# The first layer's neighbour sums of a graph kernel: from gathered rows to an edge-count matrix times a table in SBUF

## The chip, the cores and the metric

The kernel runs on one core of one Trainium2 chip, in one launch. The metric is the time of that launch on the device in microseconds (us), the median of three runs. Engines are named as in the profile: PE (TensorE matmuls), PEld (its weight loads), DVE (VectorE), ACT (ScalarE), POOL (GpSimd) and SP (SyncE, which here only issues DMAs; its rows are marked SPq).

## The reference, cut to what matters

The input is a graph with 6250 nodes, a feature row `x` of 256 floats for each node, and 206250 directed edges sorted by their destination `dst`. Two graph layers follow each other, and each has a small feed-forward part behind it. The change touches the first graph layer alone:

```python
# layer 0; feat = layernorm(x)
t1    = feat @ W1
msg   = t1[src] + feat[src] * feat[dst] @ W2
msg   = msg / (sqrt(out_deg[src]) * sqrt(out_deg[dst]))[:, None]
agg   = segment_sum(msg, dst)
embed = where(in_cnt > 0, t1 + agg, 0) + b        # leaky relu, divided by its norm
x     = x + embed
x     = x + (layernorm(x) @ Wf.T + bf)            # layer 0's feed-forward part
# layer 1: m = clifford(h[src] * r[edge_type]) * gate * norm, summed by dst, and so on
```

Every term of `agg` is linear in the source's row, and `feat[dst]` is the same for all edges of a destination. So the kernel needs for each destination only the sum, over its edges, of one table row of the source, `feat[src] / sqrt(out_deg[src])`, and a count. All multiplications with W1 and W2 come behind that sum. Layer 1 can't do this: there each edge has its own factor, the relation row `r[edge_type]`.

## The kernel before, in words

The 6250 nodes lie in 49 blocks of 128 (`NB`), node 128b + p on partition p. Each block of destinations has a window of `C` = 35 slots of 128 edges, found at run time, so there are 49 x 35 = 1715 slots a layer (`SLOTS`). A group is seven slots (`SG`); a block has five groups (`SPB`).

**Start.** DVE finds where the blocks' windows begin (L1260 to L1281), and builds one-hots for a histogram of the sources, which PE adds up (L1293 and L693); that gives the out-degrees. SP loads the edge windows (L502). Then DVE and ACT write the table (L1329, L1081), and SP stores it to HBM as `t1_d` (L510).

**First pass** (`first_pass` on PE, ACT and DVE). For each slot POOL gathers 128 table rows by an indirect DMA (`gathers`, L630) into one of 18 buffers, and after each six gathers it clears a scratch tile (L627). DVE makes a 128 x 128 f32 one-hot of the destinations (`pick_edges`, L1366), and PE multiplies the two in f32 into the block's sum in PSUM (`aggregate`, L736). Beside it the edges are put in order of their relation for layer 1: DVE ranks them (`marks`, `places`), makes one-hots of the target slot and lane (`sends`, L1449 and L1453), ACT scales the small ones by three payloads (L1109), PE moves the edges with them (`move`, L760), and `in_place` writes the result. Some groups after a block's sum is complete, its node work follows in small steps: `features`, `turn_features`, `messages`, `embeddings`, `embed_norm`, `residual`, `ffn_input`, `turn_ffn`, `feed_forward`, `fed` and `table_row`, which writes the rows of layer 1's table. X, all of x, stays in SBUF throughout.

**Second pass.** Layer 1 again gathers (POOL), multiplies each row with a relation row that PE looks up (L717, L1383), adds up by destination, and so on; behind it a top-k search and the last sum.

Each engine runs a list written out by hand: the calls in the loop over n in its `first_pass` are its order, and semaphores named `s_...` tie the lists together. A call that waits holds back all that stands behind it on its engine.

## Time and profile before

| | us |
|---|---|
| median of 3 runs | 5443.28 (5443.25 to 5448.71) |
| span of the profiled execution | 5537.5 |
| PE busy | 3805.9 (69% of the span) |
| DVE busy | 3132.6 (57%) |
| ACT busy | 1618.8 (29%) |
| POOL busy | 3849.2 (70%) |

The profiled execution is another one than the three timed runs. The page gives no time for it beside its span, which is 94.2 us above the median. Sums below are made in the time of the span, and only a difference is carried over to the median.

The first gather of layer 0 begins at 245.37 us of the span, and the last row of layer 1's table is written at 2830.9 us: the first pass takes 2586 us, the second with its end the remaining 2706 us.

### The profile page before, as it was taken

The numbers are of one execution on the slowest core, as the hardware profiler recorded it, in microseconds if no ns is written. First come the engines' busy times: TensorE is split into PE (matmuls) and PEld (weight loads), VectorE is DVE, ScalarE is ACT, GpSimd is POOL, SyncE is SP. The second block draws the span as 40 slices with busy tenths as digits, with TensorE's granted clock in tenths as the row PEclk, the third lists the DMA queues.
The fourth block names the chain that finished last, engine by engine and source line by source line (L and its number), as shares of the span: only waits on it lengthen the run. The fifth ranks groups of instructions, "written<-read, shape, count | busy, mean of one in ns | idle before, by whom it ended". The sixth has DMA issues, their size and how long they took to land.

```text
span 5537.5 us, 68744 instructions
## 1 busy us (share of the span) xinstructions
PE 3805.9 (69%) x19471; PEld 2905.8 (52%) x19471; DVE 3132.6 (57%) x12068; ACT 1618.8 (29%) x6417; POOL 3849.2 (70%) x4302
## 2 busy tenths in 40 slices
PE   6555555555556555555557887888788888888886
PEld 6444444444444444444445665656566666665654
DVE  8756565665655656555555555555455555555545
ACT  3144444544444444444420111111111111111111
POOL 0177776777777777776757777777777777777772
PEclk9577777777777777777779989999999998999988
DMA  4333333333333333333334444444444444444443
GB/s 97 117 94 97 93 99 92 99 94 98 98 97 96 96 98 93 96 95 94 95 104 116 113 111 111 113 115 112 110 115 110 115 114 110 111 110 114 112 108 76
DMA packets 278430, 572.85 MB, mean 103 GB/s; under 512 B 88622, under 2 KB 167790, under 8 KB 278056
## 3 DMA queue, kind: packets, MB, share of 16 engines
q0 software_dynamic: 164640, 456.82, 31.9%
q1 hardware_dynamic: 101576, 103.13, 6.9%
q10 hardware_dynamic: 11840, 8.50, 0.5%
q8 instruction: 164, 2.69, 0.2%
q14 instruction: 210, 1.72, 0.1%
HBM read 541.27 MB, written 26.92 MB: 103 GB/s over the span
## 4 chain that ended last, share of the span: by engine, by line
PE 42%; DVE 31%; another core or an unknown queue 16%; issue 9%; DMA 1%; ACT 0%; SPq 0%; DVEq 0%; PEldq 0%; ACTq 0%
PE psE L736 18%; DVE both L1366 8%; PE psY L717 6%; PE psT L717 6%; DVE work L1453 5%; DVE work L1449 4%; PE psE L936 3%; PE psE L917 3%; DVE work L1293 2%; PE psY L693 1%; DVE work L1383 1%; DMA acc_d<-work 1%; DVE work L1374 1%; PE psE L872 1%
## 5 line engine op out<-in xcount | busy, mean ns | idle before, releaser
L630 POOL DMA_INDIRECT work<-t_d,srci x3430 | 3271.3, 954 | 1587.8 <-issue 1155.8
L736 PE MATMUL psE<-work,both 128*128 128x257 f32 x6860 | 2219.4, 448 | 875.8 <-issue 373.7
L736 PEld LDWEIGHTS psE<-work,both 128*128 128x128 f32 x6860 | 1388.0, 225 | 1242.5 <-issue 469.2
L1109 ACT ACTIVATE work<-work 128x35 f16<-128x35 bf16 x5145 | 1133.5, 311 | 692.0 <-DVE work L1449 440.9
L1366 DVE TENSOR_SCALAR both<-iof,dstf 128x128 f32<-128x128 f32 x3430 | 813.7, 345 | 47.8 <-issue 25.7
L1449 DVE TENSOR_SCALAR work<-iob,work 128x35 bf16<-128x35 bf16 x1715 | 273.3, 269 | 806.4 <-remote 668.9
L1383 DVE TENSOR_TENSOR work<-work,psY 128x257 f32<-128x257 f32 x857 | 347.5, 420 | 631.1 <-PE psY L717 206.5
L1383 DVE TENSOR_TENSOR work<-work,psT 128x257 f32<-128x257 f32 x858 | 348.0, 420 | 601.1 <-PE psT L717 214.6
L717 PE MATMUL psT<-relb,work 126*128 126x257 bf16 x2574 | 452.1, 286 | 21.2 <-DVE work L1374 19.1
L717 PE MATMUL psY<-relb,work 126*128 126x257 bf16 x2577 | 459.8, 290 | 0.5 <-issue 0.5
L627 POOL MEMSET work<- 128x640 bf16 x571 | 380.2, 666 | 0.2
L1453 DVE TENSOR_SCALAR work<-iob,work 128x128 f16<-128x128 bf16 x1715 | 346.9, 321 | 21.0 <-issue 20.7
L717 PEld LDWEIGHTS psT<-relb,work 126*128 126x128 bf16 x2574 | 261.5, 102 | 183.8 <-issue 26.3
L717 PEld LDWEIGHTS psY<-relb,work 126*128 126x128 bf16 x2577 | 265.8, 103 | 166.3 <-issue 27.6
L917 PE MATMUL psE<-accf,work 128*128 128x256 f32 (+1 forms) x800 | 188.2, 383 | 8.3 <-DVE rstd L1517 4.3
L627 POOL MEMSET accf<- 128x640 bf16 x285 | 193.2, 678 | 0.1
L1200 ACT ACTIVATE accf<-psE,score 128x256 f32<-128x256 f32 x49 | 23.2, 473 | 568.0 <-PE psE L936 239.1
L1374 DVE TENSOR_SCALAR work<-work,tid 126x640 bf16<-126x640 f16 (+3 forms) x493 | 169.2, 388 | 13.7 <-DMA work<-types_d 13.6
L760 PE MATMUL psY<-work 128*128 128x105 f16 x1715 | 137.6, 217 | 55.5 <-issue 45.6
L693 PE MATMUL psY<-work 125*128 125x49 bf16 x1650 | 158.7, 269 | 18.1 <-DVE work L1293 17.2
L917 PEld LDWEIGHTS psE<-accf,work 128*128 128x128 f32 x800 | 149.4, 196 | 30.7 <-DVE rstd L1517 6.1
L760 PEld LDWEIGHTS psY<-work 128*128 128x128 f16 x1715 | 115.2, 102 | 95.9 <-issue 64.6
(262 smaller groups left out, 3291.1 us busy)
## 6 DMA issues: line engine op xcount, KB each, us to landing
work<-t_d,srci POOLq DMA_INDIRECT x3430
work<-types_d SPq DMA_DIRECT2D x245, 220.5 KB
both<-acc_d SPq DMA_DIRECT2D x98, 130.0 KB
t_d<-accf SPq DMA_DIRECT2D x7, 910.0 KB, 9.3
acc_d<-work ACTq DMA_DIRECT2D x1, 6370.0 KB
t_d<-accf SPq DMA_DIRECT2D x49, 130.0 KB
X<-in_x SPq DMA_DIRECT2D x1, 6144.0 KB
out<-X SPq DMA_DIRECT2D x6, 896.0 KB
```

The lines of the kernel that those rows point to most:

```text
L627: pool.memset(idle[layer], 0.0).then_inc(s_pause, 1)
L630: pool.indirect_dma_start(gath[:, n % RG, :], None, table, bass.IndirectOffsetOnAxis(ap=srci[:, n:n + 1], axis=0)).then_inc(s_g[n % RG], 16)
L717: ins = nc.tensor.matmul(psR[n % BANKS][:, 0:DW], oht[0:PT, g % 2, at, :], relb[0:PT, part, c, 0:DW], start=((c, part) == (mine[0][0], 0)) ...
L736: ins = nc.tensor.matmul(psE[:, b % 2, 0:DW], sel[:, third, k % SG, :], gath[:, n % RG, 0:DW], start=False, stop=(k == C - 1))
L760: ins = nc.tensor.matmul(psY[:, b % 2, 0:3 * C], to_q[:, n % 2, k % SG, :], to_s3[:, n % 2, k % SG, :, :].rearrange("p j s -> p (j s)"), s ...
L917: ins = nc.tensor.matmul(bank[:, i * D:i * D + many * P].rearrange("p (q n) -> p q n", n=P), f1[:, t, ht * P:ht * P + P], rows[:, t, :, :] ...
L1109: ins = nc.scalar.activation(to_s3[:, n % 2, i, j, :], to_s[:, n % 2, i, :], ACT.Copy, scale=load3[:, b // RB % 2, j, w:w + 1])
L1366: ins = v.tensor_scalar(sel[:, n % 3, i, :], iof[:, :], dstf[:, k + i:k + i + 1], None, ALU.is_equal)
L1374: ins = v.tensor_scalar(oht[0:PT, n % 2, at:at + many, :], types[0:PT, n % 2, first:first + many, :], tid[0:PT, c:c + 1], None, ALU.is_equal)
L1383: v.tensor_tensor(rows, rows, psR[n % BANKS][:, 0:DW], ALU.mult).then_inc(s_po, 1)
L1449: ins = v.tensor_scalar(to_s[:, n % 2, i, :], iob[:, 0:C], spot_s[:, b // RB % 2, w + i:w + i + 1], None, ALU.is_equal)
L1453: ins = v.tensor_scalar(to_q[:, n % 2, i, :], iob[:, :], spot_q[:, b // RB % 2, w + i:w + i + 1], None, ALU.is_equal)
```

## The change

Layer 0's gathers, the one-hots `pick_edges(0, ...)` and the f32 matmuls with them are gone. In their place:

- **A count matrix.** A block of 128 destinations is cut into 16 windows of 8 nodes (`WINS`, `NODES`). SP loads for each window up to 384 edges as three runs of 128, destinations and sources apart, from copies of both lists padded at the end (`windows`: 32 small DMAs a block). After a turn by PE (`turn_window`), DVE makes one-hots for four windows at once (`edge_hots`): of the source's low seven bits, 128 wide, and of (destination, source's block), 8 x 49 = 392 wide. PE multiplies the two (`histogram`, three matmuls a window), which gives for 8 destinations and 6272 sources how many edges join them. ACT copies the counts as bf16 into the matrix `adj` (`counts_out`).
- **The table in SBUF.** The table is no longer read from HBM. While it is made, each row is split into three bf16 parts whose sum is the f32 row (`parts_t`).
- **The sum** of a block is 49 x 3 matmuls in bf16, `adj` (128 sources x 128 destinations) times a part (`collect`).
- **Steps.** The first pass runs over 49 x 16 = 784 steps, one a window, in place of 245 groups. PE's step holds the histogram of one window and a fifteenth of the collecting of the block before.
- **Moving the edges**: `sends` makes its one-hots for 12 slots in one instruction, the scaling goes from ACT to DVE, and `move` runs three times a block.
- **X leaves SBUF** in the first pass to make room. Rows are loaded by block (`load_x`), stored to HBM (`x1_d`), and all of X is loaded back at the head of the second pass. The loads of `f1` and `f2` stand behind it, and `load_pair` stands at the end of the first pass.
- **The start**: the search for the window borders is done with a histogram of its own on PE; the gate's work on the relation rows is moved in between the one-hots.
- The fallback for edge lists that don't fit the windows keeps its own buffers.

The core of the diff:

```diff
-BURST = [6, 3]
+NODES = 8
+WINS = P // NODES
+TAKE = 3
+REACH = ((0, 8), (2, 8), (5, 8))
+FOUR = 4
+STEPS = NB * WINS
...
+            def windows(b):
+                if b >= 2:
+                    sp.wait_ge(s_wtp, b - 1)
+                sp.load(firsts, start_w[0:1, WINS * b:WINS * b + WINS])
+                for w in range(WINS):
+                    first = sp.snap(firsts[w], min_val=0, max_val=E)
+                    for r, a in enumerate((dst_p, src_p)):
+                        sp.dma_start(ints[TAKE * w:TAKE * w + TAKE, b % 2, r, :],
+                                     a[bass.ds(first, ROOMY)].rearrange("(p e) -> p e", e=P)).then_inc(s_wl[b % 2], 16)
...
-            gathers(0, t1_d)
...
+            def histogram(t):
+                n, j = t // FOUR, t % FOUR
+                bank = (psT, psY)[t % 2][:, 1, :]
+                if j == 0:
+                    pe.wait_ge(s_r, n + 1)
+                if t >= 2:
+                    pe.wait_ge(s_a, t - 1)
+                for c, (lo, hi) in enumerate(REACH):
+                    ins = nc.tensor.matmul(bank[:, lo * NB:hi * NB], hot_l[n % 2][:, c, :, j],
+                                           hot_r[n % 2][:, AT[c]:AT[c + 1], j], start=(c == 0), stop=(c == TAKE - 1))
+                ins.then_inc(s_h, 1)
+
+            def collect(b, w):
+                bank = psE[:, b % 2, :]
+                if w == 1:
...
+                    nc.tensor.matmul(bank[:, 0:DW], ident[:, :], old0[:, 0:DW], start=True, stop=False).then_inc(s_opre, 1)
+                for s in sources(w):
+                    for part, (at0, wide) in enumerate(((0, DW), (DW + 1, D), (DW + 1 + D, D))):
+                        ins = nc.tensor.matmul(bank[:, 0:wide], adj[:, b % 2, s, :], parts_t[:, s, at0:at0 + wide],
+                                               start=False, stop=(s == NB - 1 and part == 2))
...
+            def counts_out(t):
+                act.wait_ge(s_h, t + 1)
+                bank = (psT, psY)[t % 2][:, 1, :]
+                nc.scalar.copy(adj[:, b % 2, :, NODES * w:NODES * w + NODES],
+                               bank[:, 0:NODES * NB].rearrange("p (d s) -> p s d", s=NB)).then_inc(s_a, 1)
...
+            def edge_hots(n):
+                b, j = n // FOUR, n % FOUR
+                if n >= 2:
+                    dve.wait_ge(s_h, FOUR * (n - 1))
+                mine = slice(FOUR * j, FOUR * j + FOUR)
+                for c, (lo, hi) in enumerate(REACH):
+                    many = (hi - lo) * NB
+                    v.tensor_tensor(hot_r[n % 2][:, AT[c]:AT[c + 1], :],
+                                    keyed_hi[:, b % 2, c, mine].unsqueeze(1).broadcast_to([P, many, FOUR]),
+                                    ramp[:, lo * NB:hi * NB, :], ALU.is_equal)
+                v.tensor_tensor(hot_l[n % 2][:, :, :, :],
+                                keyed_lo[:, b % 2, :, mine].unsqueeze(2).broadcast_to([P, TAKE, P, FOUR]),
+                                ramp[:, 0:P, :].unsqueeze(1).broadcast_to([P, TAKE, P, FOUR]), ALU.is_equal).then_inc(s_r, 1)
...
+                link(v.tensor_tensor(to_s, four(spot_s[:, r % 2, i, some]).broadcast_to([P, THIRDS, C, FOUR]), count(C),
+                                     ALU.is_equal))
+                for j in range(3):
+                    v.tensor_tensor(to_s3[:, n % 2, :, j, :, :], to_s,
+                                    four(load3[:, r % 2, j, i, some]).broadcast_to([P, THIRDS, C, FOUR]), ALU.mult)
+                v.tensor_tensor(to_q[:, n % 2, :, :, :], four(spot_q[:, r % 2, i, some]).broadcast_to([P, THIRDS, P, FOUR]),
+                                count(P), ALU.is_equal).then_inc(s_tq, 1)
```

PE's first pass. Before, the head of a block: L728 puts in what the fallback left, L736 is the f32 sum over gathered rows, L760 moves edges, L749 and L750 rank them, L797 and L805 are node work.

```order
L728 MATMUL psE<-both,ident 128x257
L736 MATMUL psE<-work,both 128x257 x7
L760 MATMUL psY<-work 128x105 x7
L797 MATMUL psE<-ident,accf 128x128 x4
L736 MATMUL psE<-work,both 128x257 x7
L749 MATMUL psT<-work,sqj 128x280
L750 MATMUL psT<-work,sqj 128x280
L760 MATMUL psY<-work 128x105 x7
L805 MATMUL psE<-w1s,accf 128x256 x2
L805 MATMUL psE<-w2s,accf 128x256 x2
```

Now, one step and a part of the next: L959 is `histogram`, L974 `collect` (`arena` holds the three-part table, `X` the count matrix and half of the one-hots, `relw` the other half), L1056 `messages`.

```order
L959 MATMUL psY<-X 128x392
L959 MATMUL psY<-X 128x294
L959 MATMUL psY<-X 128x147
L974 MATMUL psE<-arena,X 128x257
L974 MATMUL psE<-arena,X 128x256 x2
L974 MATMUL psE<-arena,X 128x257
L974 MATMUL psE<-arena,X 128x256 x2
L974 MATMUL psE<-arena,X 128x257
L974 MATMUL psE<-arena,X 128x256 x2
L1056 MATMUL psE<-w1s,arena 128x256 x2
L1056 MATMUL psE<-w2s,arena 128x256 x2
L959 MATMUL psT<-X 128x392
```

The histograms stand between the collecting of the block before, and node work stands between both.

DVE's first pass. Before, one group with one piece of node work: seven one-hots of the destinations (L1366), then the one-hots that move seven slots (L1449, L1453), then `residual`.

```order
L1366 TENSOR_SCALAR both<-iof,dstf 128x128 x7
L1449 TENSOR_SCALAR work<-iob,work 128x35 x7
L1453 TENSOR_SCALAR work<-iob,work 128x128 x7
L1521 TENSOR_SCALAR ssq<-ssq 128x1
L1522 RECIPROCAL ssq<-ssq 128x1
L1523 SCALAR_TENSOR_TENSOR X<-accf,ssq,X 128x256
L1515 BN_STATS st<-X 128x6
```

Now, a batch of four steps: `edge_hots` (L1733, L1736), `sends` (L1843 to L1848), and `table_row` (L1959 to L1963).

```order
L1733 TENSOR_TENSOR relw<-arena 128x1568
L1733 TENSOR_TENSOR relw<-arena 128x1176
L1733 TENSOR_TENSOR relw<-arena 128x588
L1736 TENSOR_TENSOR relw<-arena 128x1536
L1843 TENSOR_TENSOR X<-relw,arena 128x420
L1846 TENSOR_TENSOR X<-X 128x3x140 x3
L1848 TENSOR_TENSOR X<-X,arena 128x1536
L1959 COPY mean<-mv 128x1
L1960 COPY arena<-degu 128x4
L1961 RECIPROCAL rstd<-rstd 128x1
L1962 TENSOR_TENSOR rdeg<-rstd,degu 128x1
L1963 TENSOR_SCALAR arena<-arena,mean,rdeg 128x256
```

The many short one-hots have become a few long ones, all with two tensors as input.

## Rows read from the trace of the kernel before

**Rows 1.** Windows: us, busy us of each engine, clock, DMA share, GB/s

```profile
100.00:200.00 100.00, 93.66 (x964) 87.47 (x961) 96.63 (x70) 0.25 (x1) 0.00 (x0) 0.67 0.08 11
245.00:2831.00 2586.00, 1467.24 (x6338) 1147.08 (x6338) 1535.45 (x7210) 1226.79 (x5555) 1829.79 (x2000) 0.75 0.36 96
2851.00:5380.00 2529.00, 2070.68 (x10945) 1527.37 (x10945) 1307.00 (x4364) 307.02 (x587) 1953.16 (x2220) 0.93 0.44 112
```

**Rows 2.** Timeline of POOL, early in both passes: start, us, line

```profile
252.73 0.65 POOL L627 MEMSET accf<- 128x640 bf16 x1
253.55 0.95 POOL L630 DMA_INDIRECT work<-t_d,srci  x1 [0.17 <-issue]
...
260.73 0.67 POOL L627 MEMSET accf<- 128x640 bf16 x1
...
2838.76 0.65 POOL L627 MEMSET work<- 128x640 bf16 x1
...
2843.02 0.65 POOL L627 MEMSET work<- 128x640 bf16 x1
```

**Rows 3.** Groups by line and form: busy us, mean ns, idle before

```profile
L736 PE MATMUL psE<-work,both 128*128 128x257 f32 x6860 | 2219.4, 448 | 875.8 <-issue 373.7 <-DVE work L1383 194.3 <-DVE both L1366 171.4
...
L1366 DVE TENSOR_SCALAR both<-iof,dstf 128x128 f32<-128x128 f32 x3430 | 813.7, 345 | 47.8 <-issue 25.7 <-remote 13.9 <-DVE dstf L1575 4.5
...
L1453 DVE TENSOR_SCALAR work<-iob,work 128x128 f16<-128x128 bf16 x1715 | 346.9, 321 | 21.0 <-issue 20.7
L1449 DVE TENSOR_SCALAR work<-iob,work 128x35 bf16<-128x35 bf16 x1715 | 273.3, 269 | 806.4 <-remote 668.9 <-PE psY L760 110.9 <-issue 26.2
```

**Rows 4.** Groups by form that price the added work

```profile
L1383 DVE TENSOR_TENSOR work<-work,psY 128x257 f32<-128x257 f32 x857 | 347.5, 420 | 631.1 <-PE psY L717 206.5 <-PE psT L717 205.7 <-remote 180.5
...
L693 PE MATMUL psY<-work 125*128 125x49 bf16 x1650 | 158.7, 269 | 18.1 <-DVE work L1293 17.2
...
L760 PE MATMUL psY<-work 128*128 128x105 f16 x1715 | 137.6, 217 | 55.5 <-issue 45.6 <-remote 9.0 <-DMA work<-t_d,srci 0.8
L1293 DVE TENSOR_TENSOR work<-work,accf 125x3840 bf16<-125x3840 bf16 x55 | 118.6, 2156 | 4.0 <-PE psY L693 2.3
...
L1293 DVE TENSOR_TENSOR work<-work,accf 125x1470 bf16<-125x1470 bf16 x55 | 50.5, 918 | 0.0
...
L1125 ACT COPY accf<-psE 128x512 f32<-128x512 f32 x49 | 28.4, 580 | 334.8 <-remote 312.1 <-PE psE L797 22.6
...
L1142 ACT COPY accf<-psE 128x256 f32<-128x256 f32 x49 | 18.0, 368 | 238.7 <-remote 199.6 <-PE psE L813 27.1 <-issue 11.9
```

**Rows 5.** Timeline of PE in the second pass, without waits

```profile
3506.28 0.50 PE L717 MATMUL psY<-relb,work 126*128 126x257 bf16 x3
3506.61 0.60 PE L736 MATMUL psE<-work,both 128*128 128x257 f32 x2
3507.04 0.50 PE L717 MATMUL psY<-relb,work 126*128 126x257 bf16 x3
```

**Rows 6.** Timeline of DVE: the start, and the first products of layer 1

```profile
41.33 20.09 DVE L1293 TENSOR_TENSOR work<-work,accf 125x3840 bf16<-125x3840 bf16 x13
...
214.99 0.21 DVE L1321 TENSOR_SCALAR degu<-psY 128x49 f32<-128x49 f32 x1 [3.07 <-PEq L706]
...
2846.36 1.03 DVE L1374 TENSOR_SCALAR work<-work,tid 126x640 bf16<-126x640 f16 x2 [13.27 <-DMA work<-types_d]
```

**Rows 7.** Timeline of SP: DMAs whose address stands in a register, and X

```profile
20.18 22.92 SPq L492 DMA_DIRECT2D X<-in_x  x1
...
46.75 0.33 SPq L502 DMA_DIRECT2D dstf<-in_dst  x1
...
48.21 0.33 SPq L502 DMA_DIRECT2D dstf<-in_dst  x1
```

More of the change, by code:

```diff
@@ L34 @@
 RG = 18
-BURST = [6, 3]
+BURST = 3
+NODES = 8
+WINS = P // NODES
+TAKE = 3
+REACH = ((0, 8), (2, 8), (5, 8))
+ROOMY = TAKE * P
+FOUR = 4
+BATCHES = NB * WINS // FOUR
+STEPS = NB * WINS
+AT = [sum(hi - lo for lo, hi in REACH[:c]) * NB for c in range(TAKE + 1)]
+TW = 3 * D + 2
+XR = 3
+THIRDS = 3
+HALF = -(-NB // 2)
+TC4 = 12
+ENOUGH = ((2, 7.0), (5, 16.0), (8, 24.0))
+MOST = 16.0
 MM = 6
@@ new lines, in program @@
+        q = o - 8 * W
+        grown = arena[:, q:q + STEPS].rearrange("p (b u) -> p b u", u=WINS)
+        q += STEPS
+        ended = arena[:, q:q + NB]
+        q += NB
+        below = arena[:, q:q + NB]
+        q += NB
+        bands = arena[:, q:q + P].rearrange("p (k u) -> p k u", k=4)
+        q += P
+        offset = arena[:, q:q + WINS]
+        q += WINS
+        inside = arena[:, q:q + WINS]
+        q += WINS
+        under = arena[:, q:q + WINS]
+        q += WINS
+        over = arena[:, q:q + NB]
@@ L250, in program @@
         assert o + 320 <= 11404
[L252 removed]
+        idle = work[:, o:o + 320].bitcast(BF16)
         late = typ[:, :].bitcast(F32)
@@ L401, in program @@
         s_scaled = sem("s_scaled")
-        s_td = sem("s_td")
+        s_td = [sem(f"s_td{k}") for k in range(2)]
         s_sel = sem("s_sel")
@@ L568, in _ @@
+            sp.wait_ge(s_part, NB)
             unordered(0)
-            sp.wait_ge(s_td, 16 * (NB // 7))
-            load_old(0, 0)
-            for b in range(NB + 2):
-                if b % 4 == 3 and b // 4 < PAIRS:
-                    load_pair(b // 4)
+            load_old0(0)
+            for b in range(NB + 3):
+                if b + 2 < NB:
+                    windows(b + 2)
+                if b >= 3:
+                    store_row(b - 3)
+                if b < NB:
+                    load_x(b)
@@ new lines, in rank_tri, with move @@
+            def rank_tri(b):
+                pe.wait_ge(s_pl, 2 * b + 1)
+                mine = marked[:, b % RB, :, :].rearrange("p c k -> p (c k)")
+                nc.tensor.matmul(psT[:, 0, 0:BINS * C], trib[:, :], mine, start=True, stop=True).then_inc(s_rp, 1)
+            def move(b, g):
+                n = THIRDS * b + g
+                pe.wait_ge(s_tq, n + 1)
+                if g == 0 and b >= 1:
+                    pe.wait_ge(s_so, b)
+                for k in third(g):
+                    i, t = k % TC4 // FOUR, k % FOUR
+                    ins = nc.tensor.matmul(psY[:, 0, 0:3 * C], to_q[:, n % 2, i, :, t], to_s3[:, n % 2, i, :, :, t],
+                                           start=(k == 0), stop=(k == C - 1))
+                ins.then_inc(s_sm, 1)
@@ new lines, in _ @@
+            for i in range(NB + 1):
+                if i < NB:
+                    t = t_rows[:, i % 14, 0:D]
+                    if i % 7 >= 4:
+                        if i >= 14:
+                            act.wait_ge(s_td[i // 7 % 2], 16 * (i // 14))
+                        nc.scalar.activation(t, X[:, i, :], ACT.Identity, scale=rdeg[:, i:i + 1],
+                                             bias=less[:, i:i + 1]).then_inc(s_arow, 1)
+                        act.wait_ge(s_arow, 3 * (i // 7) + i % 7 - 3)
+                    else:
+                        act.wait_ge(s_trow, 4 * (i // 7) + i % 7 + 1)
+                    nc.scalar.copy(parts_t[:, i, 0:D], t).then_inc(s_hi, 1)
+                if i >= 1:
+                    act.wait_ge(s_rest, i)
+                    nc.scalar.copy(parts_t[:, i - 1, DW + 1:DW + 1 + D], rest[:, (i - 1) % 3, :]).then_inc(s_mid, 1)
@@ new lines, in _ @@
+            for n in range(EN):
+                if n >= 2:
+                    dve.wait_ge(s_hmm, n - 1)
+                for one_hot, bits, wide in ((ohlo, end_lo, P), (ohhi, end_hi, NB)):
+                    ins = v.tensor_tensor(one_hot[:, n % 2, :, :],
+                                          bits[:, HG * n:HG * n + HG].unsqueeze(1).broadcast_to([NP, wide, HG]),
+                                          counted[:, 0:wide, :], ALU.is_equal)
+                ins.then_inc(s_oh, 1)
+            link(v.memset(cnt[:, :], 0.0))
@@ new lines, in _ @@
+            link(v.memset(limit[:, :], 1e9))
+            link(v.tensor_scalar(inside, offset, 0.0, None, ALU.is_ge))
+            v.tensor_scalar(under, offset, 0.0, None, ALU.is_lt)
+            link(v.memset(bands[:, :, :], 0.0))
+            for k, (nodes, most_ends) in enumerate(ENOUGH):
+                v.scalar_tensor_tensor(bands[:, k, 0:WINS], offset, float(nodes), inside,
+                                       ALU.is_lt, ALU.mult)
+                ins = v.memset(limit[32 * k:32 * k + 32, :], most_ends)
```

1002 lines of the change are left out of this document (624 added, 378 removed).

## The prediction

> **What bounds the kernel now.** I read the busy time by stretch first [rows 1]. The first pass, 245 to 2831 us, has no full engine: POOL is busy for 71% of it, DVE for 59%, PE for 57%, and TensorE is granted 0.75 of its clock. The second pass grants 0.93. Then POOL's timeline [rows 2]: six gathers and a memset take 8.00 us, 1.333 us a gather, so 1715 gathers need 2287 of the 2586 us. In the second pass three gathers take 4.26 us, 1.42 us each, 2435 of 2529 us. "POOL busy 71%" hides this, since the 0.3 us between two gathers is not counted as busy. So POOL's gathers set the pace of both passes, and the rest of the first pass (13% over POOL's need) is loss where the lists wait for each other; in rows 3 DVE's L1449 stands idle 806 us, mostly for such a wait. The change takes POOL out of the first pass. What is next is DVE or PE, and each must be summed.
>
> **The first pass, removed.** All of POOL's 2287 us. On DVE L1366 (half of 813.7 us), L1453 (346.9) and L1449 (273.3) [rows 3]. On PE the f32 matmul L736. ACT loses its scaling of the one-hots. Of DVE's 1535.4 us [rows 1] that leaves 508 us of work which stays, 10.4 us a block.
>
> **DVE, added, a block.** The nearest row is L1293, a compare of two 16-bit tensors, one of them a short row read over and over: 2156 ns for 3840 elements, 918 for 1470 [rows 4], so 0.52 ns an element; 13 in a row took 20.09 us [rows 6], which leaves 0.11 us for each instruction. `edge_hots` has 1568 + 1176 + 588 + 1536 = 4868 elements in four instructions: 3.0 us, four times a block, 12.0. `sends` has 420 + 3 x 420 + 1536 = 3216 in five: 2.3 us, three times, 7.0. The windows' bits and keys are four small instructions at some 0.2 us (L1321 [rows 6]): 0.8. The stops between chained instructions, which busy time leaves out, I put at 0.6, 5% of the kept work. Sum 12.0 + 7.0 + 10.4 + 0.8 + 0.6 = 30.8 us a block. The bounds of the unknown, the rate of runs of four elements in place of 30, are 0.52 ns and twice that, one element a cycle; I take 0.52, since element sizes and the kind of instruction are those of the row.
>
> **PE, a block, at the full clock.** Three bf16 matmuls of 257 columns are followed 0.33 us later, and an f32 one 0.43 us later [rows 5]: 0.11 us each, 0.43 ns a column. Collecting: 147 x 0.11 = 16.2. The old sum 0.43. A histogram has 833 columns, 0.36 us; its third matmul of 147 columns hides no weight load (L760's pairs took 80 ns each, 137.6 us / 1715 [rows 4]), so 0.39: sixteen are 6.3. Moves 35 x 0.08 = 2.8. Messages and feed-forward are seven f32 matmuls, 3.0; six transposes of half the width 1.3; window turn and ranks 0.6. Sum 30.6 us, the same size as DVE's. At 0.93 of the clock, which the second pass had with PE 82% busy, it is 32.9 us, and PE is the longer of the two.
>
> The histogram reads both operands at every fourth element. The trace has one matmul with spaced operands, L693, every 30th element: 96 ns for 49 columns (158.7 us / 1650) [rows 4], more than L760 takes for 105. Bounds: no charge for the spacing, 0.36 us a histogram, and 833 x 96 / 49 = 1.63 us. I take the first, since L693 is a 128-column weight load with few columns behind it, at a clock of 0.67 [rows 1].
>
> By the Trainium skill (Advanced Engine Details and Errata, SBUF Cachelines) SBUF has lines of 16 bytes, and reads keep their full rate with at least two hits on a line. Steps of 8 bytes give just two hits, steps of 60 bytes one; by that rule the first bound holds here and L693 pays, which agrees with its 96 ns, though that row can't tell spacing from weight load.
>
> **The other queues.** ACT's copy of 392 counts lies between 368 ns for 256 and 580 ns for 512 columns [rows 4], 0.48 us, 7.7 us a block, and some 3.5 us of node work: far from 33. SP issues a register-addressed DMA every 0.49 us (1.46 us for three [rows 7]); 32 window DMAs, five others and the load of 16 registers are some 20 us a block, in front of which stand waits for `store_row` and `load_old0`. They are issued a block ahead, so this hides behind 33 us, and would show above it.
>
> **How the two meet.** DVE's one-hots have two buffers, one batch of four steps ahead. DVE's batches are uneven: 3.5 us at a block's end, up to 13 with `marks`. PE's are 6.8 to 8.9. One batch of lead evens out most of it. For the losses I take what the first pass shows, 13% over its longest engine: 32.9 x 1.13 = 37.2, and say 37.5 us a block, where 52.8 was (2586 / 49). The second pass's 4% and no loss at all on full clock give the low side, 31 to 34.
>
> **The start.** In before the degrees are ready at 214.99 us [rows 6]. Added are four one-hot pairs (12.3 us) less the 11.8 us of the removed comparison, small work of some 4 us, and the gate's 7.5 us, which moves ahead of the table: 227. The table's three parts take 51 rounds. DVE has two subtractions of 256 at 0.4 us (L1383, 347.5 / 857 [rows 4]) and four rows in seven, ACT two copies and three rows in seven: 1.0 us a round if they overlap, 2.1 if not; I take 1.3, 66 us. Ranks and the first one-hots take 19, as now. First step at 313 us, some 40 us later than the first sum of before, and 68 later than the first gather.
>
> **The tail.** Behind the last histogram stand 16 steps of collecting, three blocks' node work, `within`, and the seven `parts`, each of which waits for a DMA that starts only when the one before is done, some 2.4 us on top of 2.0. I take 60 us (40 to 80). Layer 1's table is then ready at 313 + 49 x 37.5 + 60 = 2210 us in place of 2831: 621 less.
>
> **The second pass** keeps its instructions. But reloading X (6144 KB; the first load kept SP 22.9 us [rows 7]) and the 2 MB of `f1`, `f2` now stand ahead of the third load of types, which is needed at the seventh slot. DVE waits 13.3 us for the first types as it is [rows 6]. The stall is some 35 us; gathers run on, 18 ahead, so about 15 stay. None to 40 are the bounds.
>
> **Sum.** 621 - 15 = 606 us less. The sum is made in the profile's time, whose span is 5537.5; the median of the runs is 94.2 us below it. I carry the difference over: 5443.3 - 606 = 4837, say 4840 us. A microsecond more a block is 49 us.
>
> **The rivals.**
> - *No loss* (12%). The batch of lead suffices, 33.5 us a block: 4640. For it: two engines of like length and a clock that rises with PE's load. Against: both passes of before lose something.
> - *Spaced reads at half the rate* (12%). 5.7 us more a block on PE, 44 us with clock and loss: 5160. Against it only the argument on L693.
> - *The clock stays low* (12%). PE waits at each batch for DVE, and gets 0.76 as in the first pass now: 30.6 / 0.76 x 1.13 = 45.5 us a block, 5230. For it: stretches with 57% PE busy got 0.75, and even 94% busy with small matmuls got 0.67 [rows 1]. Against: collecting is dense, like the second pass.
> - *DVE's compares at one element a cycle* (6%), the case slower than before. Short rows of four may not pair as rows of 30 do. `edge_hots` would take 5.5 us and `sends` 4.0, DVE 30.8 + 10.2 + 5.0 = 46.0 us a block, with the loss 52: 5550. It decides from 49.9 us a block, where the gain of 606 us is used up ((5443 - 4837) / 49 + 37.5).
> - *Spaced reads at L693's rate* (1%), 1.63 us a histogram: near 59 us a block, 5890. *The edges don't fit the windows* and the fallback runs in both layers (under 1%): milliseconds.
>
> By the Trainium skill (VectorE: DVE Perf Modes, What auto-detection actually checks) two results a cycle need 16-bit tensors with innermost step one, and nothing is asked of a row's length; by that rule the fourth rival falls. L1293's 0.52 ns agrees for rows of 30.
>
> **How the numbers follow.** The forecast has 56%: 4840 us, by itself from 4700 to 5000. The range must reach over the first three rivals in part: 4630 to 5240. A measurement of this kernel tells some 0.2% from no change, 11 us. Faster holds all cases above the break-even of 49.9 us a block: 92%. Slower has the last rivals and what is left of their neighbours, 7%. Within 0.2%: 1%.
>
> **What the new profile would show.** POOL idle up to about 2200 us; `L959` and `L974` on PE with three 256-column matmuls in 0.33 us, and 0.4 us a histogram; `L1733` for 1568 elements at 0.93 us (1.7 would be the one-element rate) and `L1736` at 0.91; a clock of 0.9 or more in the first pass; ACT's `L1381` at 0.5 us; the first `L959` near 313 us; SP waiting, not waited for; blocks 37.5 us apart; a gap on DVE early in the second pass at the third load of types, and the same 1.42 us a gather behind it. I am wrong if the first pass shows PE waiting for window keys, so for SP; if ACT's copy out of PSUM with strides costs 1 us or more, which sums to a new bound; or if the granted clock falls.

## The result, and the profile after

The changed kernel takes 4819.12 us (median of 4, 4816.25 to 4835.1), the kernel before beside it 5443.26: a ratio of 0.886, 95% interval [0.8846, 0.8876], 624 us less. Forecast were 4840. The profiled execution is one of these runs; its span is 4816.0 us.

The windows of the new trace, with the columns of [rows 1]: us, busy us (and instructions) of PE, PEld, DVE, ACT and POOL, the granted clock, DMA share, GB/s.

```profile
100.00:200.00 100.00, 87.55 (x899) 81.75 (x897) 96.62 (x82) 3.11 (x4) 0.00 (x0) 0.52 0.27 66
295.00:2035.00 1740.00, 1729.50 (x12100) 1309.54 (x12101) 1369.78 (x3528) 488.31 (x1233) 0.00 (x0) 1.00 0.06 17
2162.00:4660.00 2498.00, 2042.72 (x10921) 1526.53 (x10921) 1309.52 (x4348) 307.79 (x587) 1954.50 (x2214) 0.93 0.44 116
```

The window of 400 to 800 us, in which the experiments below are compared:

```profile
400.00:800.00 400.00, 398.36 (x2790) 302.08 (x2790) 313.64 (x808) 110.87 (x282) 0.00 (x0) 1.00 0.06 17
```

In the first pass PE is busy 99.4% at a clock of 1.00, where it had 57% at 0.75 [rows 1]. POOL does nothing. DVE has 79%. So one engine, PE, sets the pace, and next to nothing is lost over it.

How far the blocks are apart is read from the transpose that each block issues once (L945), in PE's timeline and in the answer for that line (durations min/median/max in ns, first and last start).

```profile
306.50 0.34 PE L945 MATMUL psE<-ident,arena 48*128 48x48 f32 x1
```

```profile
L945 PE MATMUL psE<-ident,arena x49: 257/258/336, 280.5 to 2035.4; 48*128 48x48 f32 x49
```

From its second start (306.50) to its last (2035.4) lie 47 blocks: 36.8 us each; forecast were 37.5.

PE's timeline within a block (start, us from the first start to the last end, line, form of the first, count) shows what fills it.

```profile
999.73 0.90 PE L959 MATMUL psT<-relw 128*128 128x392 bf16 x3
1000.45 1.52 PE L974 MATMUL psE<-arena,X 128*128 128x257 bf16 x12
1001.81 0.91 PE L959 MATMUL psY<-relw 128*128 128x392 bf16 x3
1002.53 1.18 PE L974 MATMUL psE<-arena,X 128*128 128x257 bf16 x9
1003.55 1.35 PE L1003 MATMUL psY<-X 128*128 128x105 f16 x12
1004.72 0.53 PE L959 MATMUL psT<-relw 128*128 128x392 bf16 x1
```

Subtract starts: a histogram (L959) takes 0.72 us, where the forecast had 0.39. Twelve collecting matmuls (L974) take 1.36 us, 0.113 each; forecast 0.11. Twelve moves (L1003) take 1.17, 0.098 each; forecast 0.08.

The groups by form, 400 to 800 us (busy us, mean ns of one, idle before), price the one-hots, the copy and the histogram's three widths.

```profile
L1381 ACT CAST X<-psT 128x392 bf16<-128x392 f32 x86 | 41.8, 486 | 145.3 <-PE psT L959 145.3
...
L1733 DVE TENSOR_TENSOR X<-arena 128x1568 bf16<-128x1568 f16 x22 | 21.4, 974 | 56.7 <-PE psY L959 56.7
L1736 DVE TENSOR_TENSOR X<-arena 128x1536 bf16<-128x1536 f16 x22 | 21.0, 952 | 0.0
...
L1733 DVE TENSOR_TENSOR X<-arena 128x588 bf16<-128x588 f16 x22 | 10.1, 458 | 0.0
```

```profile
L959 PE MATMUL psT<-relw 128*128 128x392 bf16 x44 | 22.6, 514 | 0.0
...
L959 PEld LDWEIGHTS psT<-relw 128*128 128x128 bf16 x132 | 15.1, 116 | 11.3 <-issue 9.6
...
L959 PE MATMUL psT<-relw 128*128 128x147 bf16 x44 | 13.8, 313 | 0.0
```

DVE's compares with runs of four keep two elements a cycle: (974 - 458) / (1568 - 588) = 0.53 ns an element, against 0.52 in [rows 4]. The matmul's modelled end holds a fixed part, so its rate is a difference too: (514 - 313) / (392 - 147) = 0.82 ns a column, where the prediction had 0.43.

The last rows are from the timelines. DVE's row of L1673 is when the degrees are ready (compare [rows 6]). Its row of L1745 is the wait for the third load of types, early in the second pass. SP's row is the reload of X that stands ahead of that load.

```profile
221.75 0.21 DVE L1673 TENSOR_SCALAR degu<-psY 128x49 f32<-128x49 f32 x1 [2.98 <-PE psY L895]
...
2189.59 0.58 DVE L1745 TENSOR_SCALAR arena<-arena,tid 126x640 bf16<-126x640 f16 x2 [22.74 <-DMA arena<-types_d]
```

```profile
2150.47 20.82 SPq L770 DMA_DIRECT2D X<-x_d  x7
```

### The profile page after: what moved, and what is told of

The parts are those of the page before. It is cut to its first block, busy times and chain, and to the rows that moved or that the text cites. A ratio compares the mean times of both kernels' runs of the same rounds, so it can differ in the third digit from the quotient of the medians.

```text
span 4816.0 us, 76411 instructions
## 1 busy us (share of the span) xinstructions
PE 4146.2 (86%) x25967; PEld 3151.7 (65%) x25967; DVE 3100.0 (64%) x8780; ACT 938.1 (19%) x2252; POOL 2031.2 (42%) x2304
## 4 chain that ended last, share of the span: by engine, by line
PE 75%; DVE 14%; issue 5%; another core or an unknown queue 4%; ACT 1%; DMA 1%; SPq 1%; DVEq 0%; ACTq 0%
PE psE L974 15%; PE psE L932 15%; PE psY L917 6%; PE psT L917 6%; PE psY L959 6%; PE psT L959 5%; PE psY L1003 3%; PE psE L1192 3%; DVE arena L1707 3%; PE psE L1173 3%; DVE arena L1626 2%; PE psE L1056 2%; PE psY L895 2%; DVE arena L1754 1%
## 5 line engine op out<-in xcount | busy, mean ns | idle before, releaser
L816 POOL DMA_INDIRECT arena<-t_d,srci x1715 | 1639.7, 956 | 2689.6 <-issue 2547.5
L932 PE MATMUL psE<-arena 128*128 128x257 f32 x3430 | 1131.2, 413 | 289.7 <-DVE arena L1754 210.5
L974 PE MATMUL psE<-arena,X 128*128 128x256 bf16 (+1 forms) x7203 | 932.4, 275 | 0.0
L974 PEld LDWEIGHTS psE<-arena,X 128*128 128x128 bf16 x7203 | 728.9, 101 | 196.5 <-issue 0.3
L932 PEld LDWEIGHTS psE<-arena 128*128 128x128 f32 x3430 | 566.5, 203 | 407.6 <-DVE arena L1754 205.0
L1754 DVE TENSOR_TENSOR arena<-arena,psT 128x257 f32<-128x257 f32 x858 | 349.1, 420 | 601.9 <-PE psY L917 192.7
L917 PE MATMUL psT<-relw,arena 126*128 126x257 bf16 x2574 | 451.7, 286 | 19.6 <-DVE arena L1745 18.6
L917 PE MATMUL psY<-relw,arena 126*128 126x257 bf16 x2577 | 451.7, 286 | 0.3 <-issue 0.3
L1707 DVE TENSOR_SCALAR arena<-iof,dstf 128x128 f32<-128x128 f32 x1715 | 418.8, 358 | 26.3 <-remote 22.1
L813 POOL MEMSET arena<- 128x640 bf16 x571 | 382.5, 670 | 0.2
L1733 DVE TENSOR_TENSOR X<-arena 128x1568 bf16<-128x1568 f16 (+2 forms) x294 | 199.0, 732 | 250.8 <-PE psY L959 250.7
L1733 DVE TENSOR_TENSOR relw<-arena 128x1568 bf16<-128x1568 f16 (+2 forms) x294 | 198.6, 731 | 42.0 <-PE psY L959 41.2
L1745 DVE TENSOR_SCALAR arena<-arena,tid 126x640 bf16<-126x640 f16 (+3 forms) x493 | 180.3, 419 | 27.4 <-DMA arena<-types_d 27.3
L1003 PE MATMUL psY<-X 128*128 128x105 f16 x1715 | 192.8, 277 | 1.2 <-DVE X L1848 1.2
L959 PE MATMUL psT<-X 128*128 128x392 bf16 (+2 forms) x588 | 177.7, 422 | 3.2 <-DVE X L1736 3.2
L959 PE MATMUL psT<-relw 128*128 128x392 bf16 (+2 forms) x588 | 178.6, 423 | 0.4 <-DVE relw L1736 0.4
```

The costliest lines, as they stand in the source:

```text
L813: pool.memset(idle, 0.0).then_inc(s_pause, 1)
L816: pool.indirect_dma_start(gath[:, n % RG, :], None, t2_d, bass.IndirectOffsetOnAxis(ap=srci[:, n:n + 1], axis=0)).then_inc(s_g[n % RG], 16)
L917: ins = nc.tensor.matmul(psR[n % BANKS][:, 0:DW], oht[0:PT, g % 2, at, :], relb[0:PT, part, c, 0:DW], start=((c, part) == (mine[0][0], 0)) ...
L932: ins = nc.tensor.matmul(psE[:, b % 2, 0:DW], sel[:, n // SG % 3, k % SG, :], gath[:, n % RG, 0:DW], start=False, stop=(k == C - 1))
L959: ins = nc.tensor.matmul(bank[:, lo * NB:hi * NB], hot_l[n % 2][:, c, :, j], hot_r[n % 2][:, AT[c]:AT[c + 1], j], start=(c == 0), stop=(c ...
L974: ins = nc.tensor.matmul(bank[:, 0:wide], adj[:, b % 2, s, :], parts_t[:, s, at0:at0 + wide], start=False, stop=(s == NB - 1 and part == 2))
```

## Experiments: what a histogram costs

The trace has histograms at half the rate that was forecast, and a first pass as long as was forecast. The first four kernels ask for the reason of the one. They read other counts than the right ones, so their first layer's sums are wrong; the number of instructions and columns stays. They were run on one chip, beside the kernel before (5533.35 us there). The changed kernel itself was not run on that chip; the run with dense weights, whose blocks are 36.7 us apart, stands in for it below.

The moving operand read densely:

```diff
-    hot_r[n % 2][:, AT[c]:AT[c + 1], j]
+    hot_r[n % 2][:, :, :].rearrange("p n t -> p (n t)")[:, AT[c]:AT[c + 1]]
```

> Changed kernel, with the moving operand of the histogram's matmuls read from neighbouring bf16 columns (step 2 bytes) where it was read at a step of 8 bytes; weights, column counts and all other work stay. The counts, and so the first layer's sums, are those of other edges. Theory (the moving operand's step halves TensorE's rate: 833 columns of a window took 0.73 to 0.75 us at a granted clock of 1.00, the prediction had 0.39): the window's three matmuls fall to 0.35 to 0.42 us, a block from 36.8 us to 31.3 us on TensorE, VectorE (29 to 30 us of work a block) comes close behind; the kernel at 4550 to 4640 us. Rival (the weights' step of 8 bytes is what costs): no change, 4819 us, the window still 0.73 us. Rival (a fixed cost of a matmul pair, its bank or its semaphore): no change either, here and in the run with dense weights.

The weights read densely, the moving operand not:

```diff
-    hot_l[n % 2][:, c, :, j]
+    hot_l[n % 2][:, c, 0:P // FOUR, :].rearrange("p n t -> p (n t)")
```

> Changed kernel, with the weights of the histogram's matmuls read from 128 neighbouring bf16 columns instead of at a step of 8 bytes; the moving operand keeps its step of 8 bytes. The counts are those of other edges. Theory (moving operand's step): the window stays at 0.72 to 0.75 us, the weight load falls from 116 ns to about 100 ns beside it, the kernel within 10 us of 4819 us. Rival (weights' step): 0.4 us a window, 4550 to 4640 us.

The moving operand at other steps, out of the same flattened tile:

```diff
+    [:, 2 * AT[c] + j % 2:2 * AT[c + 1] + j % 2:2]          # 4 bytes
+    [:, j:8 * (AT[c + 1] - AT[c]) + j:8]                    # 16 bytes
```

> Changed kernel, with the histogram's moving operand read at a step of 4 bytes instead of 8, weights as they were. The counts are those of other edges. If the rate depends on how many columns lie in some stretch of memory, 4 bytes gives the full rate (0.39 us a window, as in the dense run); if any step over the element's own size halves it, the window stays at 0.73 us and the time at 4819 us. My forecast: the second at 60%, since the rate at 8 bytes came out at exactly two cycles a column.

> Changed kernel, with the histogram's moving operand read at a step of 16 bytes instead of 8, weights as they were. The counts are those of other edges. If the rate is one of any spaced read, the window stays at 0.73 us and the time at 4819 us; if it falls with the step, the window takes 1.4 to 1.5 us (four cycles a column), 0.7 us more, a block 36.8 + 11.4 = 48 us, the kernel 4819 + 49 x 11.4 = 5380 us. My forecast: no change at 65%.

Measured: dense 4658.51 us, ratio to the kernel before 0.842 [0.8396, 0.8446]; dense weights alone 4864.57, 0.879 [0.8765, 0.8816]; 4 bytes 4659.99, 0.842 [0.8388, 0.845]; 16 bytes 5446.42, 0.984 [0.9801, 0.9878], with blocks 48.7 us apart where the second answer said 48. In absolute time three expectations were missed, since they had been made from the 4819 us of another chip: dense is 18 us above its range, dense weights 46 above 4819 and not within 10, 16 bytes 66 above 5380. Against each other they hold: dense is 206 us faster than dense weights, and the theory said 180 to 270. The groups of L959 by form, 400 to 800 us, for the dense run, dense weights, 4 bytes and 16 bytes in turn:

```profile
L959 PE MATMUL psT<-relw 128*128 128x392 bf16 x48 | 16.0, 333 | 0.0
L959 PE MATMUL psT<-relw 128*128 128x147 bf16 x48 | 11.0, 229 | 0.0
```

```profile
L959 PE MATMUL psT<-relw 128*128 128x392 bf16 x44 | 22.5, 511 | 0.0
L959 PE MATMUL psT<-relw 128*128 128x147 bf16 x44 | 13.7, 312 | 0.0
...
L959 PEld LDWEIGHTS psT<-relw 128*128 128x128 bf16 x132 | 13.8, 106 | 12.3 <-issue 10.1
```

```profile
L959 PE MATMUL psT<-relw 128*128 128x392 bf16 x48 | 16.6, 346 | 0.0
L959 PE MATMUL psT<-relw 128*128 128x147 bf16 x48 | 11.2, 234 | 0.0
```

```profile
L959 PE MATMUL psT<-relw 128*128 128x392 bf16 x33 | 28.3, 858 | 0.0
L959 PE MATMUL psT<-relw 128*128 128x147 bf16 x33 | 14.5, 441 | 0.0
```

By the same difference over 245 columns: 0.42 ns a column dense, 0.46 at 4 bytes, 0.81 to 0.82 at 8 bytes, 1.70 at 16. All four have a granted clock of 0.99 or 1.00 there. The rate of the moving operand (bf16) about halves with each doubling of the step from 4 to 16 bytes. The weights' step is worth 10 to 18 ns a load (106 or less against 116) and nothing in time, since the loads lie beside matmuls. Both my forecasts of 60% and 65% on the steps were wrong: it is not "any spaced read", it is the step. The rivals on weights and on a fixed cost fall.

By the Trainium skill (Advanced Engine Details and Errata, SBUF Cachelines) two hits on a line of 16 bytes keep the full rate. For PE's moving operand it did not hold: two hits (8 bytes) gave half, four hits (4 bytes) the full rate.

A window of the dense run shows what a faster histogram leaves:

```profile
400.00:800.00 400.00, 381.75 (x3184) 331.25 (x3183) 352.35 (x912) 124.62 (x321) 0.00 (x0) 0.99 0.07 19
```

PE's work is 31.0 us in blocks that are 32.5 us apart (from L945, as above): now 1.5 us a block are lost, with DVE at 88%.

## Experiments: how the lists meet

If PE alone sets the pace of the changed kernel, work added to DVE is free. The large compare of `sends` done three times:

```diff
+    for _ in range(2):
+        link(v.tensor_tensor(to_q[...], four(spot_q[...]), count(P), ALU.is_equal))
```

> Changed kernel with the large compare of each third of a block's sends done three times instead of once (same result): VectorE gets 6 x 0.95 = 5.7 us more a block, 34.5 us of work in TensorE's 36.8 us. All outputs computed. Theory (TensorE alone sets the pace, the one-hots come ahead of it): under 30 us more in all. Rival (lock-step: VectorE's work in bursts reaches TensorE, as where the prediction took 13% over the busiest engine): 1.2 to 3 us a block, 60 to 150 us more.

It ran on another chip, on which the kernel before takes 5157.32 us and which I call the fast one, beside the changed kernel itself (4723.11 us): 4814.03 us, 91 more. The rival has it. The blocks are 38.7 us apart, (2128.2 - 308.72) / 47 from the two rows, with the window between:

```profile
308.72 0.34 PE L945 MATMUL psE<-ident,arena 48*128 48x48 f32 x1
```

```profile
L945 PE MATMUL psE<-ident,arena x49: 257/259/340, 280.7 to 2128.2; 48*128 48x48 f32 x49
```

```profile
400.00:800.00 400.00, 383.68 (x2654) 288.58 (x2652) 355.92 (x843) 108.08 (x273) 0.00 (x0) 0.99 0.06 16
```

DVE has 89% of 38.7 us, PE 96%; 1.9 us a block are lost that were not lost with DVE at 79%. PE's waits, 400 to 800 us (waited in total, times, longest), name the place: `turn_features` behind DVE's `features`, the rank matmuls behind `totals`, and `turn_ffn` behind `ffn_input`, not the one-hots. The three add up to 19.9 us in 10.3 blocks, the 1.9 us a block.

```profile
PEld psE L1048 <- DVE arena L1920: 10.7, 4, 2.7
...
PEld psT L993 <- DVEq L1808: 6.2, 6, 2.3
...
PEld psE L1066 <- DVE arena L1950: 3.0, 3, 1.0
```

So DVE's slack of 8 us a block is not all spare time: 5.7 us of work put into it cost 1.9 us a block.

## Experiments: what paced the kernel before

The prediction rests on POOL's 1.333 us a gather, and on 13% loss over it. The kernel before without the first layer's memsets:

```diff
-BURST = [6, 3]
+BURST = [SLOTS + 1, 3]
```

> Kernel before, without the memset that GpSimd does after each six gathers of the first layer (the second layer's stay). All outputs are computed. Theory (GpSimd's gathers set the first pass of the kernel before): a gather comes each 1.254 us where it was 1.333 us on average, 1715 x 0.08 = 137 us less, less what TensorE's and VectorE's own steps take back: 80 to 140 us less. Rival (the first pass is set by the lock-step of TensorE and VectorE, GpSimd only waits in it): under 20 us less.

On a chip that agrees with that of the first four kernels (5532.46 us for the kernel before, 5533.35 there): 5565.94 us, ratio 1.0059 [1.004, 1.0079]. GpSimd has 137 us less to do and the kernel is 0.6% slower. The theory is refuted. The rival's "under 20 us less" is nearer, but it did not foresee a loss either, and the run doesn't show its reason. POOL's waits in the first pass, of the kernel before and of this one:

```profile
POOL work L630 <- remote: 185.8, 124, 2.4
POOL work L630 <- PE psE L736: 93.5, 48, 9.9
```

```profile
POOL work L630 <- remote: 295.6, 123, 3.8
POOL work L630 <- PE psE L736: 176.3, 63, 11.3
```

What the memsets took came back as waits: 471.9 us in all against 279.3. (The trace of the kernel before is not from this chip for certain, but its span of 5537.5 us agrees with the 5532.46.) POOL's own issue was not what set the pace there. A wait is called remote where the trace ties no instruction of the core to its end, so the label doesn't say what POOL waited for. Is it the bytes? Half the row length:

```diff
+    wide = W // 2 if layer == 0 else W
+    rows = table.rearrange("n (h w) -> (n h) w", w=wide)
```

> Kernel before, with the first layer's gathers fetching rows of 130 f32 values (520 bytes) instead of 260 (the table taken as rows of half the length, the other half of the tiles zero): the same number of gathers, memsets and matmuls, half the bytes. The first layer's sums are wrong. Without the memsets GpSimd had 136 us less work and the first pass was 18 us longer, so GpSimd's issuing is not what paces it. Theory (the transfers pace it: some 1.5 us for 128 rows of 1040 bytes, and GpSimd held back in waits that the trace calls remote): the first pass falls from 2600 us to between GpSimd's own 1.333 us x 1715 = 2287 us and 2450 us, 150 to 300 us less. Rival (the lock-step of GpSimd, TensorE and VectorE over the ring of 18 gathers paces it): under 50 us less.

This one ran on the fast chip, where the kernel before takes 5157.32 us: 5151.08, ratio 0.9987 [0.9978, 0.9997]. Its first pass has no such waits at all, and takes 2608.3 (its first product) - 247.1 = 2361 us, 1.377 us a gather, where the same stretch of the kernel before takes 2851.0 - 245.4 = 2606 us in its trace:

```profile
POOL work L635 <- PE psE L741: 15.6, 42, 3.1
```

The expectation took the slower chips' waits for given, so the run doesn't decide between its two answers: where nothing holds the gathers back, there is nothing for half the bytes to win. What it does show is that on this chip its first pass stands within 4% of POOL's 1.333 us. The whole run is only 6 us shorter than the kernel before, so that kernel's first pass should stand there too; no trace of it was taken on this chip. For the slower chips this leaves open whether it is the bytes that hold the gathers back.

The changed kernel on this chip:

> The changed kernel itself, on the chip of the runs beside it: 0.886 of the kernel before by its first runs, 0.877 to 0.88 if this chip is like the one of the earlier experiments (the run with dense weights had 0.879, with TensorE's pace unchanged).

4723.11 us, ratio 0.916 [0.9144, 0.9174], which neither 0.886 nor 0.877 to 0.88 had foreseen. No wait of POOL is called remote, and the first pass is the same to 0.3 us:

```profile
L945 PE MATMUL psE<-ident,arena x49: 257/258/339, 280.2 to 2035.1; 48*128 48x48 f32 x49
...
L1754 DVE TENSOR_TENSOR arena<-arena,psY x857: 403/424/611, 2160.2 to 4631.9; 128x257 f32<-128x257 f32 x172
```

```profile
L1754 DVE TENSOR_TENSOR arena<-arena,psY x857: 403/424/604, 2162.3 to 4728.5; 128x257 f32<-128x257 f32 x172
```

The last row is the changed kernel's in the first comparison. Its second pass, which gathers, takes 2566 us there and 2472 here, and 2611 with dense weights on the chip of the first four kernels. The run with the reloads moved (below), whose first pass is that of the changed kernel, has it from 280.3 to 2035.5 us on a third chip. So a pass that gathers took another time on another chip, and the pass without gathers did not; why the chips differ, no run shows. So the change is worth 434 us here, 624 where it was first timed, and about 669 on that other chip (5533 against the 4865 of the run with dense weights).

## Experiments: versions that compute all outputs

Two f16 parts in place of three bf16 parts:

```diff
-    for part, (at0, wide) in enumerate(((0, DW), (DW + 1, D), (DW + 1 + D, D))):
+    for part, (at0, wide) in enumerate(((0, DW), (DW + 1, D))):      # adj, parts_t: F16
```

> Changed kernel, with the table in SBUF as two f16 parts where it was three bf16 parts, and the counts as f16: a third of the collecting matmuls goes (49 of 147 a block, 0.113 us each, 5.5 us), and the middle part of the table stage. All outputs are computed. Theory (TensorE sets the first pass: busy 398.4 of 400 us at a granted clock of 1.00): a block falls from 36.8 us to 31.3 us plus the 1.2 us that the run with the same TensorE work (dense moving operand) lost to the lock-step with VectorE, so 32.5 us; 49 x 4.3 = 210 us less, and some 6 us of the table stage; 0.845 to 0.85 of the kernel before. Rival (VectorE's 29 us of work and its waits set the pace as well): 35 us a block, 90 us less. Rival (f16 streams slower than bf16): no gain.

4659.18 us, 0.843 [0.8402, 0.8457], beside 5532.46 for the kernel before. The first histogram starts at 281.76 us, 13.4 earlier where the theory had some 6, and the blocks are 33.0 us apart: (1843.0 - 293.09) / 47. The theory had 32.5.

One-hots for two windows at a time in four buffers of half the size:

```diff
+    v.tensor_tensor(hot_r[n % 4][:, AT[c]:AT[c + 1], :],            # TWO = 2
+                    keyed_hi[:, b % 2, c, mine].unsqueeze(1).broadcast_to([P, many, TWO]),
+                    ramp[:, lo * NB:hi * NB, 0:TWO], ALU.is_equal)
```

> Changed kernel, with the one-hots made for two windows at a time instead of four, in four half-sized buffers: TensorE reads its moving operand at a step of 4 bytes, at which the run with that step alone took full rate. All outputs are computed. TensorE's work a block falls by 5.8 us to 31 us; VectorE has twice the compares at half the length: from 972 ns at 1568 elements and 458 at 588 a compare costs 0.52 ns an element and 0.15 us fixed, so 16 more a block are 2.4 us, 29 to 31.5 us. Theory (both engines close to each other, with the 1 us lost to lock-step): 33 us a block, 49 x 3.8 = 185 us less than 4819 us. Rival (VectorE loses its two elements a cycle where the inner row of its second input is only two elements, 4 bytes, long): a compare takes 1.7 us for 1568 elements, VectorE 43 us a block, 300 us more.

4619.2 us, 0.834 [0.8313, 0.837], beside the same 5532.46. The window of this kernel and its compare of 784 elements:

```profile
400.00:800.00 400.00, 392.48 (x3260) 330.06 (x3258) 377.57 (x1153) 128.00 (x331) 0.00 (x0) 1.00 0.07 20
```

```profile
L1736 DVE TENSOR_TENSOR relw<-arena 128x784 bf16<-128x784 f16 x51 | 28.7, 563 | 0.7 <-DVE arena L1812 0.3
```

A run of two elements keeps DVE's rate too. The blocks are 31.7 us apart ((1794.4 - 305.24) / 47) where the theory had 33, DVE is busy 94%, PE 98%: less is lost with a fuller DVE than in the dense run (88% and 95%). What differs is the lead of the one-hots, four small buffers against two large; that this is the reason was not tested alone.

The reloads of X between the types loads:

```diff
     load_types(n)
+    if n < 2 + NB // 7:
+        sp.dma_start(X[:, 7 * (n - 2):7 * (n - 2) + 7, :], x1_d...).then_inc(s_xl, 16)
```

> Changed kernel, with the seven reloads of X (and the two weight loads of the last stage) issued one behind each types load of the second pass, where all seven stood ahead of the third types load. All outputs are computed. Theory (the 22.74 us that VectorE waits for the third types load at 2166.9 us is the queue of those reloads, and GpSimd stops 20.84 us for it): 15 to 21 us less. Rival (the wait only spreads over the next types loads, each behind one reload): under 5 us less.

4844.81 us, 0.877 [0.8742, 0.8791], against 0.879 [0.8765, 0.8816] of the run with dense weights, which ran on another chip with the same time for the kernel before: by the ratios unclear. By the traces, DVE's wait of 24 us at the third types load is gone, and the second pass, from its first to its last product, is 12.5 us shorter than in that run (2159.4 to 4757.5 against 2157.7 to 4768.3). That is under the theory's 15 and over the rival's 5, and no clear effect: in the two traces of the kernel before with and without memsets, the same untouched second pass differs by 10 us (2599 and 2609).

All together, the one-hots of four windows in one batch but laid out in pairs:

```diff
+    keys = keyed_hi[:, b % 2, c, mine].rearrange("p (h t) -> p h t", t=2)
+    v.tensor_tensor(hot_r[n % 2][:, :, AT[c]:AT[c + 1], :],         # p h n t, h = t = 2
+                    keys.unsqueeze(2).broadcast_to([P, 2, many, 2]),
+                    ramp[:, lo * NB:hi * NB, 0:2].unsqueeze(1).broadcast_to([P, 2, many, 2]), ALU.is_equal)
```

> Changed kernel with three edits, all outputs computed: the one-hots of four windows still in one batch, but the moving operand laid out in pairs of windows, so that TensorE reads it at a step of 4 bytes; two f16 parts in place of three bf16 parts; the reloads of X between the types loads. TensorE's work a block 31.0 us (from the dense run: 381.75 of 400 us, 32.5 us a block) less 5.5 = 25.5 us. VectorE's compares keep their number and length, 28.8 us of work a block (313.64 of 400 us at 36.8 us). Theory (VectorE is now the bound and the lock-step with TensorE costs some 1 to 2 us over it): 30 to 31 us a block, 49 x 6.3 = 310 us less, 6 of the table stage and 13 of the reloads: 4490 us where the changed kernel takes 4819, a ratio to it of 0.932. Rival (the compare loses its two elements a cycle in the pair layout, whose inner row is two elements): VectorE 12 us more, 41 us a block, slower than the changed kernel. Rival (a loss of 13% over the busiest engine, as the prediction had it): 32.5 us a block, 4590 us.

4414.15 us, against 4723.11 of the changed kernel on the same chip (309 less, a ratio of 0.935 where the theory had 0.932) and 5157.32 of the kernel before: 0.856 [0.8542, 0.857]. Its window:

```profile
400.00:800.00 400.00, 350.26 (x2648) 288.65 (x2646) 364.20 (x947) 128.47 (x332) 0.00 (x0) 0.93 0.07 20
```

The blocks are 31.5 us apart, not 30 to 31: no engine is full (DVE 91%, PE 88%), the clock fell to 0.93, and PE waits for DVE's node work. PE is busy for 27.6 us of a block, where the theory had 25.5; at 0.93 of the clock 25.5 would be 27.4. The waits below, of `turn_ffn`, `turn_features` and the rank matmuls, are 52.7 us in 12.7 blocks, 4.1 us each. So PE's 5.5 us of work less bought only 0.2 us a block over the run with two windows in four small buffers (31.7).

```profile
PEld psE L1068 <- DVE arena L1941: 23.8, 12, 2.4
...
PEld psE L1050 <- DVE arena L1911: 16.5, 8, 3.6
...
PEld psT L995 <- DVEq L1802: 12.4, 4, 3.4
```

By these waits the order of the node work in the two lists is the next thing to tune; no run tried it.

## Why the prediction came out right

4840 was 21 us off, but the step that sized the first pass held two errors that cancel, and the carried difference of 94.2 us hid a third. The mechanism was right, and the closeness of the number is luck.

- *POOL leaves, PE is next*: right. PE 99.4% busy, DVE 79%.
- *PE 30.6 us a block at the full clock*: mis-sized. The term "I take the first" for the histogram, 0.39 us, measured 0.72: 16 x 0.33 = 5.3 us a block. L693's slow columns were put down to its weight load and its clock, which left the spacing without a price; the spacing costs. Moves at 0.098 in place of 0.08 add 0.6. 30.6 + 5.9 = 36.5, measured 36.8. The rival "spaced reads at half the rate", given 12%, was true in its mechanism; its 5160 us was not, because it also carried the clock and the loss.
- *Clock 0.93 and 13% loss*: wrong, neither cost anything. The clock was 1.00 in the window, and 0.6% was lost. The 13% had been read off the kernel before as a loss "where the lists wait for each other". Most of it was POOL held back in its gathers: of the 299 us over POOL's need POOL waited 279 in the profiled execution (185.8 of it called remote), and on the chip without remote waits, with the same two lists and rows of half the length, the first pass had 1.377 us a gather, 3% over its need. That loss leaves with the gathers. The lock-step does cost something once DVE is near 88% (1.5 us a block in the dense run, 1.9 with the added load), but at 79% it cost 0.2 us or less. With the true histogram and the prediction's clock and loss a block would have been its own rival's 44 us.
- *DVE 30.8 us*: 313.64 us of each 400 are 28.9 us of busy time. The 0.52 ns an element held, so the fourth rival, the slower side, fell. The rule of the Trainium skill (VectorE: DVE Perf Modes, What auto-detection actually checks) agrees: it asks for 16-bit tensors with step one, not for long rows, and rows of four and of two kept the rate here.
- *ACT 0.48 us a copy*: 0.486. *SP hidden*: no wait on it in the first pass's rows.
- *Start 313 us*: the degrees came at 221.75 (forecast 227) and the first histogram at 295.18. *Tail 60*: 295.2 + 49 x 36.8 = 2098, and layer 1's table is ready at 2139.9: 42. *Stall of 35 us, of which 15 stay*: DVE waited 22.74, and POOL stopped for 20.8 (longest wait of L816), so the gathers that run 18 ahead hid little of that stop. What it costs in the end is less: without it the second pass was 12.5 us shorter, not clear of the differences between executions, where the prediction had 15.
- *The difference of 94.2 us between span and median, carried over*: here the sum was lucky. Layer 1's table came 691 us earlier (621 forecast) and the passes behind it were 31 us shorter (15 longer forecast): 116 us better than forecast in the time of the two spans, of which 94 and another 3 go back. The first 70 us are the prediction's own error: 18 in the start, 34 in 49 blocks, 18 in the tail. The other 46 are most likely a difference of chips: the span of 5537.5 us lies within the 5514 to 5556 us that the kernel before takes on the two slower chips, not near the 5443 beside which the change was timed. Set against the run with dense weights, on one of those two, the stretch from the first product to the end grows from 2686.5 to 2700.1 us, the 15 us longer that were forecast. So on such a chip the change is worth about 669 us where 606 were forecast, and the 4840 came close because the kernel before was timed on a chip that gathers faster than the one in its profile. Which chip each of them ran on is not known, so this stays an inference.
- *The rival at L693's rate*: its sum gives (30.6 + 19.8) / 0.93 x 1.13 = 61 us a block, not 59; nothing else rests on it.

The 12% for half rate was too little for a price that no row gave.

## What to carry to other kernels

Price a matmul by the step of its moving operand: in bf16 4 bytes were nearly free here (0.46 ns a column against 0.42), and each doubling to 8 and 16 about halved the rate. A layout that suits the engine that writes (runs of four for VectorE) may cost the engine that reads; a run of two suited both.

A percentage of loss belongs to a cause. Before it is carried to a new schedule, ask which wait holds it, and whether this wait is among the things that the change removes.

Where a change removes gathers, its worth can differ from chip to chip (434 to 669 us here); give ratios with the chip's own run of the kernel before, and know on which chip a profile was taken before its span is used in a sum.

## What the runs showed of the hardware that I had not expected

- PE's rate by the moving operand's step: 0.42, 0.46, 0.82 and 1.70 ns a column at 2, 4, 8 and 16 bytes. A weight load: 116 ns at 8 bytes, 106 or less dense, about 100 at 4 bytes, all hidden.
- The same kernel took 5157 us on one chip, 5443 in the first comparison, and 5532 and 5533 on two others, and its gathering passes hold the difference: 2472, 2566 and 2611 us for the same 1715 gathers of layer 1 in the changed kernel, against a first pass without gathers that agrees to 0.3 us between the first two of these.
- Fewer memsets between gathers made the kernel slower by 0.6% on a chip where gathers wait: POOL's waits rose from 279.3 to 471.9 us. Why it lost and not only broke even stays open.
